# Attention heads turned by 32x32 blocks on VectorE, and a new order of the work between score visits

## The reference

```
xn = layernorm(x)
q, k, v = (xn @ Wq.T, xn @ Wk.T, xn @ Wv.T), each split into 16 heads of 16
A = tril(1 + q.k/4 + (q.k/4)**2/2), per head        # the Taylor features multiplied out
y = A @ v ;  y = y / (row sum of A) ;  attention = y @ Wo.T
ffn: softmax over the 2 best of 8 experts, out = sum of weight * (silu(xn W1) * (xn W2)) W3
out = x + attention + ffn
```

## Time and profile before

| | |
|---|---|
| median of 3 runs | 626.68 us (625.76 to 627.82) |
| the profiled execution: its time | 631.28 us |
| its span, first to last instruction | 629.5 us |
| TensorE busy | 599.8 us, 95% |
| VectorE busy | 467.4 us, 74% |
| ScalarE busy | 334.1 us, 53% |
| GpSimd busy | 359.7 us, 57% |
| granted TensorE clock, mean | 0.996 of full speed |

### The profile page before, as it was taken

How to read it: one execution, slowest core, us unless ns; L and a number is a source line. 1 busy time by engine, 2 the same in 40 slices (tenths; PEclk the granted TensorE clock), 3 DMA queues, 4 the chain that set the end, 5 groups by cost and what they waited for, 6 DMA issues and landing times.

```text
span 629.5 us, 16824 instructions
## 1 busy us (share of the span) xinstructions
PE 599.8 (95%) x5063; PEld 467.2 (74%) x5063; DVE 467.4 (74%) x1193; ACT 334.1 (53%) x483; POOL 359.7 (57%) x453
## 2 busy tenths in 40 slices
PE   8899999999999999998999899999999999999994
PEld 8665666767666666665788688888888888887884
DVE  6877878787878676588797477777777777777772
ACT  3668878787878677765564232333333323323331
POOL 4256463737364654557068456566666566666655
PEclk9999999999999999999999999999999999999998
DMA  4653554546544444553953567877777777777763
GB/s 134 173 130 104 124 173 108 162 104 163 125 103 124 96 130 102 160 146 104 360 112 60 126 144 159 159 160 153 156 151 157 157 142 160 153 152 150 165 119 43
DMA packets 107333, 88.13 MB, mean 140 GB/s; under 512 B 46352, under 2 KB 95376, under 8 KB 107248
## 3 DMA queue, kind: packets, MB, share of 16 engines
q1 hardware_dynamic: 73136, 54.59, 33.8%
q0 software_dynamic: 16704, 28.12, 23.3%
q10 hardware_dynamic: 17408, 4.33, 3.2%
HBM read 27.72 MB, written 22.95 MB: 80 GB/s over the span
## 4 chain that ended last, share of the span: by engine, by line
PE 48%; SPq 20%; DVE 13%; issue 9%; DMA 5%; POOL 3%; ACT 2%; POOLq 1%; DVEq 0%; ACTq 0%
SPq L481 13%; PE banks L1372 11%; PE banks L1242 10%; SPq L363 7%; PE banks L1223 6%; PE banks L1262 6%; PE banks L1271 4%; PE banks L1393 4%; DMA out<-yo,xw 2%; PE banks L1306 2%; PE banks L1291 1%; DVE yw L861 1%; PE banks L1332 1%; DMA xq<-xg 1%; POOL xg L592 1%
## 5 line engine op out<-in xcount | busy, mean ns | idle before, releaser
L618 POOL DMA_INDIRECT out<-yo,xw x71 | 112.6, 1585 | 46.1 <-DVE yo L1160 33.3
L564 POOL TENSOR_SCALAR_AFFINE_SELECT T<-T 128x512 f32<-128x512 f32 x128 | 81.0, 643 | 100.7 <-ACT T L655 48.7
L1372 PE MATMUL banks<-w12h,xgh 128*128 x284 | 114.0, 401 | 6.1 <-ACT xgh L747 5.3
L592 POOL DMA_INDIRECT xg<-xs_scr,glist x71 | 72.7, 1024 | 81.0 <-DMA xq<-xg 60.8
L774 ACT ACTIVATE hs<-banks 128x512 f32<-128x512 f32 x71 | 42.4, 598 | 142.3 <-DMA hq<-hs 67.8
L1372 PE MATMUL banks<-w12h,xgl 128*128 x284 | 113.0, 398 | 0.6 <-DVE xgl L1132 0.5
L1372 PE MATMUL banks<-w12l,xgh 128*128 x284 | 111.2, 392 | 0.0
L655 ACT ACTIVATE T<-banks 128x1024 f32<-128x1024 f32 x64 | 62.1, 1023 | 29.9 <-PE banks L1223 28.4
L559 POOL DMA_INDIRECT xs_scr<-xb,slots x64 | 63.6, 993 | 20.5 <-issue 12.4
L1242 PE MATMUL banks<-T,vau 128*17 128x512 f32 (+3 forms) x1024 | 75.2, 434 | 0.0
L1176 DVE TENSOR_TENSOR hs<-banks,hs 128x512 f32<-128x512 f32 x71 | 48.9, 689 | 30.9 <-PE banks L1372 24.9
(11 more groups left out here) (187 smaller groups left out, 1230.9 us busy)
## 6 DMA issues: line engine op xcount, KB each, us to landing
hq<-hs SPq DMA_DIRECT2D x244, 64.0 KB
w12r<-w SPq DMA_DIRECT2D x16, 512.0 KB, 5.6
Q<-Q SPq DMA_DIRECT2D x126, 64.0 KB, 2.4
out<-xa SPq DMA_DIRECT2D x16, 256.0 KB
w3r<-w SPq DMA_DIRECT2D x8, 512.0 KB, 7.7
K<-Kt SPq DMA_DIRECT2D x126, 32.0 KB
xq<-xg SPq DMA_DIRECT2D x118, 32.0 KB
xq<-xg ACTq DMA_DIRECT2D x118, 32.0 KB
```

The costliest lines, as they stand in the source:

```text
L564: e.affine_select(out=v, in_=v, pattern=[[0, 4], [1, P]], compare_op=ALU.is_ge, fill=-1.0, base=0, channel_multiplier=-1).then_inc(s["g_mk ...
L592: e.indirect_dma_start(xg[:, t % GR, :], None, xs_d, bass.IndirectOffsetOnAxis(glist[:, t:t + 1].bitcast(U32), 0)).then_inc(s[f"d_g{t % GR ...
L618: e.indirect_dma_start(out, bass.IndirectOffsetOnAxis(xw[:, t % XR, NE:NE + 1].bitcast(U32), 0), yo[:, t % 2, :], None, compute_op=ALU.add ...
L1372: i = e.matmul(banks[:, 2 * (t % 2) + m, :], a[:, k, :], w[:, bass.ds(expert[t] * 4 + (2 * k + m), 1), :], start=(k == 0 and n == 0), stop ...
```

## The change

The steps t and y go. VectorE gets two functions in place of `copy_yw` and `normalise`. `rows_of(n)` adds CT to bank 4, turns the 128x512 result by 32x32 blocks, takes the reciprocal of the row sums and multiplies. `heads_of(b, g)` turns two visits' normalised heads back by 32x32 blocks into the tile yT in SBUF; ScalarE's `y_high` and VectorE's `y_low` split it. The small constant is added with CT, and the rows of Wo are reordered on the host to fit. The lists `slot_a`, `slot_b` and `slot_c` are written anew: in a steady batch visit 0 has C, c2 | T, c3, x0, x1 of the next batch, r; visit 1 has c0, v0; visit 2 has c1, v1 | v2, o0 of the batch before; visit 3 has v3, o1. On VectorE, `norm_x` of the next batch moves ahead of c2's low part, the x low parts run in visit 1 behind `places`, both `top` run in visit 3 with `both`, and the `w12_low` units are spread otherwise. Two fillers become longer (8 in place of 5, in visits 1 and 2 of batch 7), and two of 4 are new (visits 2 and 3 of batch 0). In the END list t and y go too. The last scatters of a batch are sent in the same batch. At the seam the two `o` steps of the last batch run behind the first expert's `up`.

```diff
-W12_WITH = {(1, 1): 0, (1, 2): 1, (2, 1): 2, (2, 2): 3, (3, 1): 4, (3, 2): 5, (4, 1): 6, (4, 2): 7, (7, 0): 8}
-W12_LOW_WITH = {(1, 2): 0, (1, 3): 1, (2, 2): 2, (2, 3): 3, (3, 2): 4, (3, 3): 5, (4, 2): 6, (4, 3): 7}
+W12_WITH = {(1, 2): 0, (2, 2): 1, (2, 3): 2, (3, 2): 3, (4, 2): 4, (4, 3): 5, (5, 2): 6, (6, 2): 7, (7, 0): 8}
+W12_LOW_WITH = {(1, 3): 0, (2, 3): 1, (3, 1): 2, (3, 3): 3, (4, 3): 4, (5, 1): 5, (5, 3): 6, (6, 3): 7}
...
 def slot_a(n):
-    b, qd = divmod(n, 4)
-    if n == 0:
-        return [("C", 0, 0), ("f", 1, 6)]
-    return [("x", b + 1, 0), ("x", b + 1, 1)] if qd == 1 and 0 < b < LAST else []
+    return [("C", 0, 0), ("f", 1, 6)] if n == 0 else []
 def slot_b(n):
     b, qd = divmod(n, 4)
     if qd == 0:
-        steps = [("T", b, 0), ("c", b, 3 if b == 0 else 2)]
-    elif b == LAST:
-        steps = [("o", b - 1, qd - 1)] if qd < 3 else []
-    elif qd == 1:
-        steps = [] if b else [("v", 1, 0)]
-    elif qd == 2:
-        steps = [("c", b + 1, 1)]
-    else:
-        steps = [("o", b - 1, 0)] if b else []
-    if n == NQ - 1:
-        steps.append(("f", n, 4))
-    return steps + ([("t", (n - 1) // 4, (n - 1) % 4)] if n else []) + ([("G", 0, 0)] if n == NQ - 1 else [])
+        return [("T", 0, 0), ("c", 0, 3)] if b == 0 else [("C", b, 0), ("c", b, 2)]
+    if b == LAST:
+        return [("f", n, 4), ("G", 0, 0)] if qd == 3 else [("f", n, 8)]
+    if qd == 1:
+        return [("c", b + 1, 0), ("v", b + 1, 0)]
+    if qd == 2:
+        return [("c", b + 1, 1), ("v", b + 1, 1)]
+    return [("v", b + 1, 3)] + ([("o", b - 1, 1)] if b else [("f", n, 4)])
 def slot_c(n):
     b, qd = divmod(n, 4)
     if n == 0:
         return [("r", 0, 0), ("x", 1, 0), ("x", 1, 1)]
     if qd == 0:
-        return [("c", b, 3), ("y", b - 1, 1), ("r", b, 0)]
-    if b == LAST:
-        return [("y", b, 0)] if qd == 3 else [("f", n, 5)]
-    if qd == 3:
-        return ([("o", b - 1, 1)] if b else []) + [("y", b, 0), ("C", b + 1, 0)]
-    return ([("c", b + 1, 0)] if qd == 1 else []) + [("v", b + 1, i) for i in range(2 * qd - 2, 2 * qd) if b or i]
+        return [("T", b, 0), ("c", b, 3)] + ([("x", b + 1, 0), ("x", b + 1, 1)] if b < LAST else []) + [("r", b, 0)]
+    if qd == 2:
+        return ([("v", b + 1, 2)] if b < LAST else []) + ([("o", b - 1, 0)] if b else [("f", n, 4)])
+    return [("o", b - 1, 1)] if n == NQ - 1 else []
 def sends_after(n, m):
@@ -92,17 +82,15 @@
     if m == 2:
         return None
     k = 3 * qd + min(m, 2)
-    if k == 0:
-        return (b - 1, 7, 8) if b else None
     i = k - (3 if b == LAST else 5)
     if b == LAST and i >= 5:
         return {5: (b, 5, 7), 6: (b, 7, 8)}.get(i)
-    return (b, i, i + 1) if 0 <= i < 8 else None
+    return (b, i, i + 1 if i < 6 else 8) if 0 <= i < 7 else None
-END = (("f", NQ, 4), ("t", LAST, 3), ("f", NQ, 3), ("y", LAST, 1), ("f", NQ, 2), ("o", LAST, 0), ("o", LAST, 1))
+END = (("f", NQ, 4), ("f", NQ, 3), ("f", NQ, 2), ("o", LAST, 0), ("o", LAST, 1))
...
+            def y_high(b, k):
+                e.wait_ge(s["v_yb"], 2 * b + k + 1)
+                if b:
+                    e.wait_ge(s["p_o"], 2 * b)
+                e.activation(yTh[:, k, :], yT[:], ACT.Copy).then_inc(s["a_yt"], 1)
...
+                if qd == 1 and b < LAST:
+                    step("x", b + 1, 0)
+                    step("x", b + 1, 1)
+                elif b and qd % 2 == 0:
+                    y_high(b - 1, qd // 2)
...
-            def copy_yw(n):
+            def rows_of(n):
                 e.wait_ge(s["p_av"], n + 1)
+                if n:
+                    e.wait_ge(s["v_yt"], n)
+                done(e, "T", n // 4, 0)
+                e.tensor_tensor(yw.rearrange("p (i m) -> p i m", i=4), banks[:, 4, :].rearrange("p (i m) -> p i m", i=4),
+                                CT[:, n % 4, :].unsqueeze(2).to_broadcast([P, 4, P]), ALU.add).then_inc(s["v_yw"], 1)
+                e.wait_ge(s["v_yw"], n + 1)
                 if n >= 2:
-                    e.wait_ge(s["p_t"], n - 1)
-                done(e, "T", n // 4, 0)
-                e.tensor_tensor(yw[n % 2].rearrange("p (i m) -> p i m", i=4), banks[:, 4, :].rearrange("p (i m) -> p i m", i=4),
-                                CT[:, n % 4, :].unsqueeze(2).to_broadcast([P, 4, P]), ALU.add).then_inc(s["v_yw"], 1)
-            def normalise(b, qd):
-                n = 4 * b + qd
-                u = n % 2
-                y4 = bank("t", b, qd).rearrange("p (i r c) -> p i r c", i=4, r=4)
-                e.wait_ge(s["p_t"], n + 1)
-                e.tensor_scalar(rd[:, u], y4[:, :, :, 16], 2e-12, None, ALU.add).then_inc(s["v_rd"], 1)
-                e.wait_ge(s["v_rd"], 2 * n + 1)
-                e.reciprocal(rd[:, u], rd[:, u]).then_inc(s["v_rd"], 1)
-                e.wait_ge(s["v_rd"], 2 * n + 2)
+                    e.wait_ge(s["v_yn"], n - 1)
+                e.transpose(yt[n % 2][:], yw[:]).then_inc(s["v_yt"], 1)
+                e.wait_ge(s["v_yt"], n + 1)
+                e.reciprocal(rd[:, n % 2], yt[n % 2].rearrange("p (k c) -> p k c", c=32)[:, :, 16]).then_inc(s["v_rd"], 1)
+                b, qd = divmod(n, 4)
+                g = qd // 2
+                e.wait_ge(s["v_rd"], n + 1)
                 if b:
-                    e.wait_ge(s["p_y"], 2 * (b - 1) + qd // 2 + 1)
-                i = e.tensor_tensor(yn[:, :, 64 * qd:64 * qd + 64].rearrange("p i (r c) -> p i r c", r=4), y4[:, :, :, 0:16],
-                                    rd[:, u].unsqueeze(3).to_broadcast([P, 4, 4, 16]), ALU.mult)
-                release(i, "t", b, qd)
+                    e.wait_ge(s["v_yb"], 2 * (b - 1) + g + 1)
+                e.tensor_tensor(yn[:, g, :, 16 * (qd % 2):16 * (qd % 2) + 16],
+                                yt[n % 2].rearrange("p (k c) -> p k c", c=32)[:, :, 0:16],
+                                rd[:, n % 2].unsqueeze(2).to_broadcast([P, 16, 16]), ALU.mult).then_inc(s["v_yn"], 1)
+            def heads_of(b, g):
+                e.wait_ge(s["v_yn"], 4 * b + 2 * g + 2)
+                if 2 * b + g:
+                    e.wait_ge(s["v_yl"], 2 * b + g)
+                e.transpose(yT[:], yn[:, g].rearrange("p k c -> p (k c)")).then_inc(s["v_yb"], 1)
+            def y_low(b, k):
+                e.wait_ge(s["a_yt"], 2 * b + k + 1)
+                e.tensor_tensor(yTl[:, k, :], yT[:], yTh[:, k, :].bitcast(F32), ALU.subtract).then_inc(s["v_yl"], 1)
...
-                    i = e.tensor_copy(CT[:], bank("T", b, 0)[:, 0:P].rearrange("p (q i) -> p q i", q=4)[:, :, 0:4])
+                    e.wait_ge(s["c_eps"], 1)
+                    i = e.tensor_scalar(CT[:], bank("T", b, 0)[:, 0:P].rearrange("p (q i) -> p q i", q=4)[:, :, 0:4],
+                                        eps[:, 0:1], None, ALU.add)
...
                     gates(b)
+                    if b < LAST:
+                        norm_x(b + 1)
                 elif n == NQ - 3:
                     tiles()
                 elif n == NQ - 2:
                 elif qd == 2:
                     if b < NBATCH - 2:
                         variance(b + 2)
-                    if (b, qd) in W12_LOW_WITH:
-                        w12_low(W12_LOW_WITH[b, qd])
-                elif qd == 3 and b < LAST:
-                    top(b + 1, 1)
-                    if b < NBATCH - 2:
-                        rsqrt(b + 2)
+                elif qd == 3 and b < NBATCH - 2:
+                    rsqrt(b + 2)
...
-                elif qd == 0 and b < LAST:
-                    norm_x(b + 1)
+                elif qd == 3:
+                    top(b + 1, 0)
...
-                elif qd == 2 and b < LAST:
-                    top(b + 1, 0)
                 elif qd == 3 and b < LAST:
+                    top(b + 1, 1)
                     both(b + 1)
...
+                b, qd = divmod(n, 4)
                 if n:
-                    copy_yw(n - 1)
-                if n % 4 == 1 and n // 4 < LAST:
-                    places(n // 4)
+                    rows_of(n - 1)
                 for item in slot_a(n):
                     step(*item)
+                if qd == 1 and b < LAST:
+                    places(b)
+                    step("x", b + 1, 0)
+                    step("x", b + 1, 1)
+                elif b and qd % 2 == 0:
+                    y_low(b - 1, qd // 2)
                 before_b(n)
                 items = slot_b(n)
                 if n % 4 in (0, 2) and n // 4 < LAST:
...
+                if qd == 3:
+                    heads_of(b, 0)
+                elif qd == 1 and b:
+                    heads_of(b - 1, 1)
                 after_c(n)
-            copy_yw(NQ - 1)
-            step("t", LAST, 3)
+            rows_of(NQ - 1)
+            y_low(LAST, 0)
...
-            step("y", LAST, 1)
+            heads_of(LAST, 1)
             w12_low(UNITS)
-            step("o", LAST, 0)
+            y_low(LAST, 1)
...
-                elif kind == "t":
-                    n = 4 * b + k
-                    e.wait_ge(s["v_yw"], n + 1)
```

(31 more changed lines are left out.)

26 lines of the change are left out of this document (12 added, 14 removed).

## The result

The changed kernel takes 717.84 us (median of 4, 716.46 to 719.71); the kernel before, on the same chip, 626.22 us (625.48 to 627.82). The ratio is 1.146 [1.143, 1.150]: 91.6 us slower. The prediction said slower, by 39.4 us, with 683 as the upper end of its range. The direction was right and the size far too small.

The account below looks back on a forecast made before the run. TensorE bounded the old first stage; VectorE was to become busiest, its late releases holding TensorE. Six batches 37.4 us more, batch 0 0, seam 2: 39.4 more, the median from 626.7 to about 666 us, range 634 to 683.

Parts of the forecast that it names:

- The three waits: TensorE waits for c2's low part before x (about 4 us), x low before c0 (3), c1's low part before o0 (2 or less).
- the walk: Steady batch followed visit by visit through TensorE's and VectorE's lists: 40.75 us in place of about 34.5; six batches 244.3.
- VectorE's lag into visit 0: VectorE's work of visit 3 ends late, so it enters visit 0 6.1 us behind TensorE.
- The turn: New 128x512 turn by 32x32 blocks on VectorE: 0.75 us with its gap, bounds 0.61 and 0.9.
- Rival B: TensorE stays near its bound or VectorE sets the pace without waits: 16 us less, about 611; chance 0.11.
- A: Same mechanism half hidden, only visits 3 and 0 lose: 3.3 us a batch, 20 in six, about 646; chance 0.20.
- D: No change within 0.3%: VectorE's waits happen to equal TensorE's saving, 627; chance 0.04.
- C: New turns cost 0.9 us or more, or GpSimd's contention lengthens VectorE's work: 16 us more, about 682; chance 0.10.
- One sign of being right: In batches 1 to 6 TensorE's busy time falls to about 31 us each while the batch grows to about 40.
- Batch 0: It has no y and no o, and VectorE's lag is taken up before batch 1: 0 us more.
- From batch 7 to the first expert matmul: VectorE gets 4 us more work and the last two o steps end behind the late heads_of: 2 us more.
- The second failed step: VectorE's other pieces, such as norm_x, top, gates, places and place_rows, were put at their durations in the earlier trace.

Follow-up runs that it names:

- E1: Changed kernel with 14, 12 and 8 filler matmuls on TensorE in its waits before x0, c0 and o0: 694.87 us, 1.109.
- E9: Changed kernel with the turned rows written to bank 4 in PSUM in place of SBUF: 716.12 us in 2 runs, 1.140.
- E8: E5 with w12_low units spread over batches 1 to 6 and y_low on GpSimd for all batches but the last: 656.27 us, 1.039.
- E2: Changed kernel's VectorE turns, lists and VectorE's work in the old kernel's order, rows_of whole, heads_of right behind it: 648.32 us, 1.035.
- E5: E2 with rows_of cut, its later part where normalise stood; heads_of behind it in visit 0 and at visit 2's end: 639.72 us, 1.015.
- E10: E5 with c2's low part ahead of the turn, multiplication and heads_of in visit 0: 626.47 us in 12 runs, 0.998.
- E11: E10 with the larger copy of each v step on ScalarE in place of VectorE: 633.4 us, 1.008.
- E12: E10 with only heads_of behind c2's low part in visit 0, the rest of rows_of ahead of it: 627.68 us in 12 runs, 1.000.

## Why the prediction was right in direction and wrong in size

**Right.** The reason for the sign: a bank that TensorE needs is released by VectorE, in order, and the new list has more work in front of each release. The three waits stood where the walk put them. They were up to 4.1, 4.1 and 3.4 us long, against "about 4", 3 and "2 or less", and 59.3 us in six batches, against the 58.5 (6 x 9.75) for which the walk has TensorE idle. (The walk's own times give the first wait 4.95, from 8.3 to 13.25, and not 4.) VectorE's lag into visit 0 was 7.0 us against 6.1: its addition began at 157.31 in batch 3, whose first score matmul began about 150.3. VectorE still waits for `attend`, 5.03 us in visit 1 and 3.43 in visit 3. Timeline of VectorE in batch 3, changed kernel:

```profile
157.31 0.68 DVE L864 TENSOR_TENSOR yw<-banks,CT 128x512 f32<-128x512 f32 x1
158.03 0.71 DVE L869 STREAM_TRANSPOSE yt<-yw 128x512 f32<-128x512 f32 x1
...
159.06 0.77 DVE L877 TENSOR_TENSOR yn<-yt,rd 128x256 f32<-128x256 f32 x1
...
170.47 0.69 DVE L864 TENSOR_TENSOR yw<-banks,CT 128x512 f32<-128x512 f32 x1 [5.03 <-PE banks L1260]
...
172.23 0.42 DVE L877 TENSOR_TENSOR yn<-yt,rd 128x256 f32<-128x256 f32 x1
...
173.92 0.55 DVE L969 SCALAR_TENSOR_TENSOR gap<-off,cum 128x8 f32<-128x8 f32 x1
174.50 1.29 DVE L895 TENSOR_TENSOR xTl<-banks,xTh 128x512 fp32r<-128x512 f32 x2
```

The turn costs 0.71 us, as in the earlier trace rows; with its gap 0.74, for a forecast of 0.75. Rival B's estimate of 1.24 us, worked out from the Trainium skill's bf16 figure for VectorE, is far above that for this fp32 turn, and the measurement decides. That VectorE's turn is the fastest for 32x32 blocks stands in the Trainium skill, page "VectorE: DVE Perf Modes", section "Rules for kernel authors", not in the section that rival B names. Of the rivals, A (646), B (611) and D (627) were too low. C was nearest in size (its 2.4 us a batch make 14.4 in six, not 16), but not by its first cause: the turns were not dearer. Its second cause, GpSimd beside VectorE, did occur, in `top` and others, while `norm_x` and `place_rows` became shorter.

One sign of being right failed: TensorE's busy time was to fall to about 31 us a batch and rose to 36.3 (217.84 for six). It is the clock that hides the saving. In E1, at 0.99 of it, TensorE without its fillers is busy for 31.7 a batch (239.90 less 49.43, over six).

**The sum of the miss.** 39.4 us were forecast and 85.2 came, on the profiled executions: 45.8 short. The prediction's terms against the runs:

- Six batches at full clock: 244.3 in the walk, 263.6 in E1. Short by 19.3.
- TensorE's clock: no term in the walk; 285.7 less 263.6 of E1 is 22.1. This is the largest failed step. The walk used durations for c, x and o, taken in batches where TensorE never waited longer than 0.9 us, and put them behind waits of up to 4 us without asking whether they hold there. It did so while it had TensorE idle for over 9 us in each batch of 40.
- Batch 0, put at 0: 3.2, of which one part is the clock again (0.94 in that stretch).
- From batch 7 to the first expert matmul, put at 2: 5.6 (46.6 against 41.0). The second stage, put at 0: 2.4 less (326.9 against 329.3). With batch 0 short by 4.4 together.

Where the 19.3 arise can be read in batch 2 of E1, 43.7 us against 40.75: VectorE comes to `rows_of` 7.0 us into visit 0 (walk 6.1) and is through c2's low part at 14.4 (13.25). It is through x0's low part 7.8 us into visit 1 (6.9), and through c1's at 20.4 (18.95), counted from the same start. Up to each of these points VectorE's list takes longer than its rows said.

**The second failed step: the durations of VectorE's other pieces.** The walk took them all from the earlier trace rows. That holds only while an instruction keeps its operands and its company. Groups of VectorE in the kernel before (busy us, mean ns of one), then the same in E1, which has the changed kernel's order at full clock:

```profile
L964 DVE TENSOR_TENSOR eq<-oh,rk 128x32 f32<-128x32 f32 x16 | 6.5, 407 | 0.3
L928 DVE TENSOR_TENSOR eq<-eq,i8m 128x32 f32<-128x32 f32 x16 | 6.5, 404 | 0.6
L927 DVE TENSOR_TENSOR eq<-L,m 128x32 f32<-128x32 f32 x16 | 3.4, 210 | 0.5
L948 DVE TENSOR_TENSOR xb<-xb,eq 128x32 f32<-128x32 f32 x8 | 1.5, 191 | 0.3
L959 DVE SCALAR_TENSOR_TENSOR gap<-off,cum 128x8 f32<-128x8 f32 x8 | 1.3, 167 | 0.3
```
```profile
L877 DVE TENSOR_TENSOR yn<-yt,rd 128x256 f32<-128x256 f32 x30 | 16.5, 550 | 1.0
...
L938 DVE TENSOR_TENSOR eq<-eq,i8m 128x32 f32<-128x32 f32 x16 | 8.7, 544 | 0.5
L937 DVE TENSOR_TENSOR eq<-L,m 128x32 f32<-128x32 f32 x16 | 5.8, 364 | 0.6
L969 DVE SCALAR_TENSOR_TENSOR gap<-off,cum 128x8 f32<-128x8 f32 x8 | 4.0, 504 | 0.3
...
L958 DVE TENSOR_TENSOR xb<-xb,eq 128x32 f32<-128x32 f32 x8 | 3.4, 427 | 0.3
L974 DVE TENSOR_TENSOR eq<-oh,rk 128x32 f32<-128x32 f32 x16 | 3.0, 187 | 0.3
```

The multiplication `yn` takes 550 ns in place of 424. `places` has a `gap` of 504 ns in place of 167, `gates` an addition of 427 in place of 191, `top` two steps of 364 and 544 in place of 210 and 404. One piece, `place_rows`, became shorter, 187 in place of 407. Instructions with the same operands got longer in one list and shorter in another, so their place in time decides, and what stands beside them there is GpSimd's work. The changed kernel, GpSimd first, and a step of `top` that belongs to the first row:

```profile
150.95 0.98 POOL L550 DMA_INDIRECT xs_scr<-xb,slots  x1 [0.16 <-issue]
...
158.34 1.22 POOL L555 TENSOR_SCALAR_AFFINE_SELECT T<-T 128x512 f32<-128x512 f32 x2 [2.69 <-ACT T L646]
...
173.23 1.22 POOL L555 TENSOR_SCALAR_AFFINE_SELECT T<-T 128x512 f32<-128x512 f32 x2 [2.59 <-ACT T L646]
```
```profile
151.27 0.70 DVE L937 TENSOR_TENSOR eq<-L,m 128x32 f32<-128x32 f32 x1
```

The multiplication at 159.06 began while masks ran and took 0.77 us; the one at 172.23 ended before 173.23 and took 0.42. `gap` at 173.92 is under a mask again and ends at 174.47, the mask at 174.45; the step of `top` ends at 151.97, GpSimd's scatter instruction at 151.93. A long small piece lasts until GpSimd's instruction is through. The Trainium skill, page "SBUF — State Buffer", section "Who interferes with whom", describes such a thing: VectorE with two inputs from SBUF and GpSimd reading SBUF share a port, and the one that has it keeps it to the end of its instruction. The trace agrees: 424 or 425 ns with a PSUM source in all 64 executions of the kernel before and E9, up to 921 with two SBUF sources. For the multiplication E9 shows that two SBUF sources are needed. For the small pieces no run changed the operands; the evidence is that their ends coincide with GpSimd's, and that more work on GpSimd made them longer still, up to 3.17 us (E8). From the rows shown: 30 multiplications at 126 ns more are 3.8 us, the two steps of `top` 2.4 and 2.2, `gates` 1.9, `gap` 2.7, and `place_rows` 3.5 less; with the step before `gap` (`cum`, 471 ns in place of 156) 2.5 more. That is 12 us over eight batches, some 9 in these six against the 19.3, though not all of it lies on the path. The rest, in gaps between dependent instructions and in pieces that the walk estimated, wasn't separated.

**How much was the order.** The old order with the new turns (E2) loses 21 us against its own runs of the kernel before, the old order with the later half where `normalise` stood (E5) 8, and with c2's low part ahead of that (E10) nothing. So the turns on VectorE cost nothing when the later half of `rows_of` stands behind what the others wait for, which in visit 0 is c2's low part too, and the 92 us come from where the lists put the pieces and what they moved. They gain nothing measurable either: of TensorE's 7 us in six batches 4 turn into waits. From E10 on, moving load off VectorE (E11) or changing the order a little (E12) gave no more, and no version was found that beats both kernels by a measurable amount.

## What to carry to other kernels

Time freed on the busiest engine is worth something only if the engine that gets the work still reaches its releases in time: walk its list in order from the start of a stage to each release, and put the later half of a new piece behind the releases. Where such a walk gives TensorE waits of some microseconds per batch, add a term for matmuls at half the clock behind them; here it was about as large as the rest of the miss. And durations of two-operand VectorE instructions hold only for their place: one that moves under GpSimd's work, or whose source moves from PSUM to SBUF, can double, and in E8 a piece of 0.19 us took 3.17. So work given to GpSimd to relieve VectorE can cost VectorE more than it takes away.
